# Two-layer cross-attention and FFN network: the second layer's query path staged ahead of the batch loop, with the key rotation on another engine

## Chip, core and metric
One core of a Trainium2 chip. The metric is the device time of one execution in microseconds (us). TensorE is called PE (its weight loads PEld), VectorE DVE, ScalarE ACT, GpSimd POOL, SyncE SP.

## What is computed
`x` is (8, 100, 256), `ctx` (8, 1444, 64). Layer 0 is a causal cross-attention with 16 small heads and a top-1 expert FFN with a shared expert. Layer 1, which the change touches, is below (16 heads, K = 128, query width 192, key width 64); layernorms stand ahead of each block and residuals behind. In the kernel all weights behind the rotation are merged beforehand: `wqb`, `wqt` (query, 128 and 64 of the 192 rows), `amat` (rotated query to 64 latent values that meet the rotated keys), `bmat` (output).

```python
q = (hidden_q @ Wq.T) per head;  q_big = rope(q @ w_kc_q)        # 192 wide
kv_r = rope(kv_c);  q_r = q_big @ W_qr;  k_r = kv_r @ W_kr
scores = q_r @ k_r.T
attn = softmax(scores);  out = (attn @ values(kv_r)) @ Wo.T
x = x + out;  then the FFN of quantised activations and ternary weights
```

## The kernel before
Five instruction streams are written out by hand, one per engine, with semaphores (`wait_ge`, `then_inc`); each engine runs its stream in order. Layer 0, the experts (L1042, L1055) and the merging of weights take the first 255 us. Then comes the stage ahead of layer 1's loop: keys of batch 0 are turned (`turn_keys`, `low_keys`), the shared expert's output is added (`shared_out`, L1008, and `second_residual`), the routed output gathered from DRAM is added (`third_input`, L1923), each batch is normalised (`norm_x3`, with GpSimd's power L636 in between) and turned (`turn_x3`), and the first two units' queries are made.

A unit u is one batch b = u // 2 and one half of the heads (8 heads, 800 query columns). The loop runs over 16 units of 24 slots. In each slot PE computes `scores` (L1197, one of 12 key tiles by 400 query columns, a pair of single-record matmuls: high part and low part), ACT takes the exponent (L1674), and GpSimd adds the weights up, one add of 800 columns per two slots (`add_weights`, L614). Slots 1 to 21 also hold one of 21 `max_chunk`s (L1177) of the next unit, which DVE reduces (L1976); `max_chunk` m waits until reduce m - 2 is done, since there are two banks. Behind slots 7, 15 and 23 stand four `values` each (L1209), a burst on PE of some 2.9 us. `sum_weights`, a reciprocal through DRAM scratch (`spread_sums` on SP), `divide` (L1997, slot 15) and `attention_out` (L1232, slots 17 to 20 of even units) belong to the unit or batch before, as does the FFN: `quantise_x` behind slot 23 of even units, `gate` and `up` in odd ones, `hidden` and `max_h` (L2044) at the end of odd ones. `turn_max` (L1183) at slot 23 ends a unit's slots.

The query path, for unit u + 2 inside unit u: `q_big` (24 matmuls of 100 columns, L1116 and L1121, at slots 1, 3, 5 and 9, 11, 13), `rope` on DVE (L1943, L1947, slots 7 and 15), `q_latent` (24 matmuls, L1143, slot 23), then ACT's `keep_q` (high part, L1592) and DVE's `low_q` (the rest, L1957) in the first slot of the next unit. `turn_x3` and `norm_x3` of batch b + 2 are in the loop too. GpSimd rotates the keys of batch b + 2 (`rotate_keys`, four instructions L594 to L597 for two of 12 tiles, behind slots 7, 15, 23, 31, 39, 47 of batch b). SP loads the raw keys, stores and loads the sums, places the maxima (`place_max`) and stores the output.

Of the kernel before, what the change touches and what calls it, by code (L numbers as in the profile page):

```python
# [84 lines left out]
X_SLOT, NORM_SLOT = 39, 31  # L85
# [11 lines left out]
ROTATE_SLOT = (7, 15, 23, 31, 39, 47)  # L97

# [19 lines left out]
def key_rows(t):  # L118
    return KP if t < KL else KP - 1
# [40 lines left out]
def build(nc, x, ctx_in, wq0, wkv0, wout0, router, gate_up, down, sh_gate, sh_up, sh_down,  # L160
          wq1, kcq, kckv, wqr, wkr, wo1, fg, fu, fd, lnw, rope_q, rope_kc, rope_ks, out):
    with ExitStack() as ctx:
# [30 lines left out]
        ropeq = place("ropeq", [128, 4, S])  # L193
# [76 lines left out]
        assert cursor[0] <= after_qb  # L270
        cursor[0] = after_qb
# [48 lines left out]
        edn = [place(f"edn{i}", [128, FM, D]) for i in range(EBUF - 1)]  # L320
        hs = place("hs", [128, FM, T])
# [21 lines left out]
        for i in range(2):  # L343
# [54 lines left out]
        var2_ready, rstd2_ready, xn2_ready, xn2_turned, xn2_kept = (  # L398
            sem("var2_ready"), sem("rstd2_ready"), sem("xn2_ready"), sem("xn2_turned"), sem("xn2_kept"))
# [102 lines left out]
        def place_max(sp, u):  # L502
# [17 lines left out]
        def _(sp):  # L520
# [64 lines left out]
        def rotate_keys(pool, step, b, j):  # L585
# [1657 lines left out]
```

## Time and profile before

| what | us |
|---|---|
| median of three runs | 905.37 |
| lowest, highest | 898.53, 906.08 |
| profiled execution: span from first to last instruction | 903.0 |
| first scores of the loop | 306.1 |

The profile is one execution on the chip. Busy times of PE rest on modelled ends and overlap, so differences of starts are the surer measure. An fp32 matmul shows as two records. PEclk is the granted clock as a share of 2.4 GHz: 1.00 or 0.50.

### The profile page before, as it was taken

How to read it: one execution, taken by the hardware profiler on the slowest of the kernel's cores; microseconds unless marked ns; L12 is line 12 of the kernel's file. 1: busy time of each engine (PE TensorE's matmuls, PEld its weight loads, DVE VectorE, ACT ScalarE, POOL GpSimd, SP SyncE). 2: the span in 40 equal slices, each digit the busy share in tenths (PEclk: the TensorE clock that was granted, in tenths of full speed). 3: DMA queues.
4: the chain of work that ended last, by engine and by line, in shares of the span. 5: the costliest groups of instructions: out<-in, count | busy, mean ns of one | idle time of the engine just before them, and what ended most of it. 6: DMA issues, size and time to landing. Idle time of an engine off the chain costs nothing.

```text
span 903.0 us, 15604 instructions
## 1 busy us (share of the span) xinstructions
PE 826.4 (92%) x5844; PEld 606.6 (67%) x5844; DVE 585.3 (65%) x1133; ACT 397.2 (44%) x883; POOL 453.2 (50%) x465
## 2 busy tenths in 40 slices
PE   4998879999998799999999999999999999999883
PEld 3566656788887667677667677676767766765442
DVE  3437864213358675677878778778787787786545
ACT  2248852222231454544544454454354454444441
POOL 3000002800041187768776876776776776567630
PEclk9979996999999899999999999999999999999986
DMA  9532022789810100000000100000000000000000
GB/s 212 187 123 89 2 67 79 261 299 317 299 46 10 35 1 12 18 10 10 19 10 1 31 10 2 10 26 7 10 23 10 10 6 10 2 16 10 2 13 11
DMA packets 42168, 52.28 MB, mean 58 GB/s; under 512 B 12230, under 2 KB 35704, under 8 KB 41836
## 3 DMA queue, kind: packets, MB, share of 16 engines
q1 hardware_dynamic: 41068, 49.63, 17.5%
q0 software_dynamic: 1024, 1.64, 0.6%
q8 instruction: 47, 0.77, 0.3%
q14 instruction: 29, 0.24, 0.1%
HBM read 45.80 MB, written 5.36 MB: 57 GB/s over the span
## 4 chain that ended last, share of the span: by engine, by line
PE 68%; DVE 13%; ACT 7%; DMA 5%; issue 5%; SPq 1%; POOL 0%; POOLq 0%; ACTq 0%; DVEq 0%
PE ps L1197 14%; PE ps L1209 10%; PE ps L1177 7%; PE ps L1116 6%; PE ps L1121 3%; PE ps L1232 3%; DMA xs<-xs_scratch 3%; PE ps L1042 3%; PE ps L994 3%; PE ps L1143 3%; ACT sm L1465 2%; PE ps L1055 2%; DVE xyz L1947 2%; DVE xyz L1943 1%; PE ps L893 1%
## 5 line engine op out<-in xcount | busy, mean ns | idle before, releaser
L614 POOL TENSOR_TENSOR acc<-acc,pt 120x800 f32<-120x800 f32 (+1 forms) x157 | 299.1, 1905 | 94.4 <-ACT pt L1674 61.4
L1674 ACT ACTIVATE pt<-ps 120x400 f32<-120x400 f32 (+1 forms) x384 | 190.1, 505 | 222.5 <-PE ps L1197 211.6
L1976 DVE TENSOR_REDUCE nm<-ps 128x1 f32<-128x482 f32 (+1 forms) x336 | 213.7, 655 | 100.3 <-PE ps L1177 98.1
L1197 PE MATMUL ps<-qh,khl 128*120 128x400 f32 (+1 forms) x384 | 157.9, 411 | 11.1 <-ACT pt L1674 8.3
L1209 PE MATMUL ps<-pt,kv 120*64 120x400 f32 (+1 forms) x768 | 143.8, 510 | 0.0
L1177 PE MATMUL ps<-khl,qh 128*128 128x482 f32 (+1 forms) x336 | 131.6, 393 | 5.3 <-DVE nm L1976 4.6
L1197 PE MATMUL ps<-ql,kh 65*120 65x400 f32 (+1 forms) x384 | 134.3, 350 | 0.0
L1197 PEld LDWEIGHTS ps<-qh,khl 128*120 128x120 f32 (+1 forms) x384 | 70.9, 185 | 58.6 <-issue 32.4
L1209 PEld LDWEIGHTS ps<-pt,kv 120*64 120x64 f32 (+1 forms) x768 | 51.9, 138 | 65.8 <-issue 55.8
L636 POOL TENSOR_TENSOR rstd<-veps,mhalf 100x1 f32<-100x1 f32 (+2 forms) x20 | 13.4, 670 | 158.1 <-DVE veps L1808 114.6
L1197 PEld LDWEIGHTS ps<-ql,kh 65*120 65x120 f32 (+1 forms) x384 | 71.3, 186 | 5.1
L1116 PEld LDWEIGHTS ps<-x3T,wqb 128*128 128x128 f32 x512 | 68.3, 195 | 3.1 <-issue 0.7
L614 POOL TENSOR_TENSOR acc<-pt,pt 121x800 f32<-121x800 f32 x16 | 30.6, 1910 | 77.0 <-ACT pt L1674 77.0
L1177 PEld LDWEIGHTS ps<-khl,qh 128*128 128x128 f32 (+1 forms) x336 | 60.1, 179 | 12.6 <-DVE nm L1976 8.9
L1116 PE MATMUL ps<-x3T,wqb 128*128 128x100 f32 x512 | 67.3, 275 | 0.7 <-ACT x3T L1429 0.5
L1042 PE MATMUL ps<-xsT,egu 128*128 128x128 f32 x448 | 52.6, 276 | 1.0 <-DVE hs L1900 0.6
L1042 PEld LDWEIGHTS ps<-xsT,egu 128*128 128x128 f32 x448 | 51.9, 192 | 1.8 <-ACT xsT L1429 1.3
L1592 ACT ACTIVATE qh<-ps 64x400 fp32r<-64x400 f32 x64 | 31.9, 499 | 46.6 <-PE ps L1143 46.1
L689 POOL DMA_INDIRECT xn<-ys_scratch,slot x8 | 8.5, 1067 | 78.2 <-DMA ys_scratch<-ysb 76.2
L1947 DVE TENSOR_TENSOR xyz<-ps,ropeq 64x200 f32<-64x200 f32 x128 | 46.2, 361 | 1.3
L1908 DVE TENSOR_TENSOR hT<-sg,ps 128x512 f32<-128x512 f32 x14 | 9.6, 686 | 48.2 <-PE ps L1042 48.2
L1232 PE MATMUL ps<-bmat,ct 128*100 128x256 f32 x128 | 33.5, 385 | 6.4 <-DVE ct L1997 5.8
(277 smaller groups left out, 1246.0 us busy)
## 6 DMA issues: line engine op xcount, KB each, us to landing
egu<-_L_ffn_gate_up_proj_dram SPq DMA_DIRECT2D x14, 1024.0 KB, 6.0
edn<-in_L_ffn_down_proj_dram SPq DMA_DIRECT2D x14, 512.0 KB, 7.1
spread<-inv_scratch SPq DMA_DIRECT2D x30, 100.0 KB, 2.7
craw<-in_ctx_dram SPq DMA_DIRECT2D x8, 360.0 KB
wo_n<-in_L_xattn_Wo_dram SPq DMA_DIRECT2D x1, 2048.0 KB, 10.5
wq_n<-in_L_xattn_Wq_dram SPq DMA_DIRECT2D x1, 2048.0 KB, 8.0
xs_scratch<-zero SPq DMA_DIRECT2D x1, 1792.0 KB, 9.9
xs<-xs_scratch SPq DMA_DIRECT2D x14, 128.0 KB, 6.1
```

The source lines that it names most:

```text
L614: nc.gpsimd.tensor_tensor(total[r, :, :], before[r, :, :], pt[j % PT_BUF][r, :, :], ALU.add).then_inc(p_added, 1)
L994: last = mm(ps[:, 2 * (k % 2) + a, 0:HT], sgu[:, c, a, 128 * m:128 * m + 128], xnT[:, c, HT * n:HT * n + HT], start=c == 0, stop=c == DC - 1)
L1042: last = mm(ps[:, 2 * (t % 2) + a, TR * m:TR * m + TR], egu[t % EBUF][:, c, FI * a + 128 * m:FI * a + 128 * m + 128], xsT[t % 2][:, c, :], ...
L1116: mm(ps[:, q_bank(u, a), S * part:S * part + S], wqb[:, c, h, 0:128], x3T[:, c, :], start=c == 0, stop=c == DC - 1)
L1177: mm(ps[0:w, 3 + m % 2, 0:MN], qh[u % 2][:, 128 * i:128 * i + w], khl[b % 2][:, MSTART[n]:MSTART[n] + MN], start=True, stop=True).then_inc ...
L1197: last = mm(ps[0:key_rows(t), k % 2, 0:HT], lhs[:, keys], rhs[:, HT * a:HT * a + HT], start=first, stop=not first)
L1209: last = mm(ps[CD * a:CD * a + CD, 2, 0:HT], kv[b % KV_BUF][r, t, :], pt[j % PT_BUF][r, a, :], start=t == 0, stop=t == KT - 1)
L1232: last = mm(ps[0:S, 6, 0:D], ct[:, S * i:S * i + S], bmat[:, i, :], start=i == 0, stop=i == GH - 1)
L1592: last = nc.scalar.activation(qh[u % 2][p:p + CD, HT * a:HT * a + HT], ps[CD * a:CD * a + CD, 5, 0:HT], ACT.Copy)
L1674: nc.scalar.activation(pt[j % PT_BUF][0:rows, k % 2, :], ps[0:rows, k % 2, 0:HT], ACT.Exp).then_inc(p_ready, 1)
L1947: last = tt(o[CD * j:CD * j + CD, 2, e:HG:2, :], ps[CD * e:CD * e + CD, bank + 1, 0:HT // 2].rearrange("p (i q) -> p i q", i=HG // 2), rop ...
L1976: nc.vector.tensor_reduce(nm3[0:w, i, n:n + 1], ps[0:w, 3 + m % 2, 0:MN], AX.X, ALU.max).then_inc(m_reduced, 1)
```

## The change
The query path leaves the loop. It runs ahead of it in eight quads: `quad(n)` gives g (four batches), p (half of the heads) and e (which half of these). A quad is two `q_tail` (L1121's part, two matmuls of 400 columns each), four `q_main` (two each), four `rope`s on DVE (two 128x400 products each; the 64-row tail goes through ACT's `keep_tail` and GpSimd's `rope_tail`), and `q_latent` of the quad before (12 matmuls of 400 columns). `keep_q` and `low_q` write `qhi`, `qlo`; `store_q` writes them to DRAM scratch in four DMAs per quad, `load_q` reads one unit in three (two copies of the high part, one of the low part), into three buffers `qh`, `ql`. `load_q(0)` and `load_q(1)` stand on SP behind `store_q(3)`, `load_q(u + 2)` at the head of unit u. All eight x3 are made ahead of the loop. `max_chunk`s of unit 0 stand in quads 4 to 6. In the loop DVE rotates the keys at the slots where GpSimd did.

```diff
-X2_LATE, X2_DONE, PT_LATE = (2, 3, 4), 9, 2 * 7
-QB_AT = (1, 3, 5)
+HB = B // 2
+QUADS = 2 * NU // HB
+QBUF = 3
+MAIN_BANK, TAIL_BANK, LATENT_BANK = (0, 1), (6, 7), (2, 5)
+TERNARY_IN, X3_IN, MAX_IN = (0, 0, 2, 2, 3, 3), (1, 1, 2, 2), (4, 5, 6)
...
+def quad(n):
+    return n // 4, n // 2 % 2, n % 2
...
+        def store_q(sp, n):
+            g, p, e = quad(n)
+            sp.wait_ge(q_hi, 2 * n + 2)
+            sp.wait_ge(q_lo, 2 * n + 2)
+            heads = q_dram.rearrange("(g b p) l d (a e n) -> g p l a e d b n", g=2, b=HB, p=PAIRS, a=2, e=2)
+            for l, src in enumerate((qhi[e], qlo[e])):
+                for a in range(2):
+                    sp.dma_start(heads[g, p, l, a, e],
+                                 src[CD * a:CD * a + CD, :, :, :].rearrange("d b i s -> d b (i s)").bitcast(F32)).then_inc(q_stored[e], 16)
+        def load_q(sp, u):
+            n = 2 * PAIRS * (u // PAIRS // HB) + 2 * (u % PAIRS)
+            for e in range(2):
+                sp.wait_ge(q_stored[e], 64 * (n // 2 + 1))
+            if u == QBUF - 1:
+                sp.wait_ge(latent_done, 2 * QUADS)
+            elif u >= QBUF:
+                sp.wait_ge(s_done, LANE * (u - QBUF + 1))
+            for p in (0, CD):
+                sp.dma_start(qh[u % QBUF][p:p + CD, :].bitcast(F32), q_dram[u, 0]).then_inc(ld_q[u % QBUF], 16)
+            sp.dma_start(ql[u % QBUF][0:CD, :].bitcast(F32), q_dram[u, 1]).then_inc(ld_q[u % QBUF], 16)
...
-            place_max(sp, 0)
+            for n in range(4):
+                store_q(sp, n)
+            load_q(sp, 0)
+            load_q(sp, 1)
             sp.wait_ge(fq_turned, 6)
...
+            store_q(sp, 4)
+            store_q(sp, 5)
+            place_max(sp, 0)
+            store_q(sp, 6)
+            store_q(sp, 7)
             for u in range(NU):
                 b = u // PAIRS
+                if u + 2 < NU:
+                    load_q(sp, u + 2)
...
+            def rope_tail(n, a, i):
+                m = 4 * n + 2 * a + i
+                pool.wait_ge(tail_kept, m + 1)
...
+                nc.gpsimd.tensor_tensor(zt[m % 8][:, :].rearrange("p (b q) -> p b q", b=HB), tail2[i][:, :].rearrange("p (b q) -> p b q", b=HB),
+                                        ropeq[:, 2, :].unsqueeze(1).to_broadcast([128, HB, S]), ALU.mult).then_inc(z_ready, 1)
...
+            for e in range(2):
+                pool.wait_ge(q_stored[e], 64 * QUADS // 2)
...
-                    if b + 2 < B and s in ROTATE_SLOT:
-                        rotate_keys(pool, step, b + 2, ROTATE_SLOT.index(s))
...
+            def q_tail(n, a):
...
+                for c in range(DC):
+                    last = mm(ps[:, TAIL_BANK[a], 0:HT], wqt[:, c, h:h + 2, :].rearrange("p h q -> p (h q)"),
+                              x3T[:, c, HT * g:HT * g + HT], start=c == 0, stop=c == DC - 1)
...
+            def q_main(n, a, i):
+                g, p, e = quad(n)
+                m = 4 * n + 2 * a + i
+                if m >= 2:
+                    pe.wait_ge(rope_done, m - 1)
+                h = 2 * HG * p + HG * a + 2 * e + i
+                for c in range(DC):
+                    last = mm(ps[:, MAIN_BANK[i], 0:HT], wqb[:, c, h, 0:128], x3T[:, c, HT * g:HT * g + HT],
+                              start=c == 0, stop=c == DC - 1)
+                last.then_inc(main_done, 1)
...
                 if c == 0:
-                    pe.wait_ge(q_hi, u + 1)
+                    pe.wait_ge(ld_q[u % QBUF], 48 * (u // QBUF + 1))
...
+            for n in range(QUADS):
+                q_tail(n, 0)
+                q_tail(n, 1)
+                if n:
+                    q_latent(n - 1)
+                for a in range(2):
+                    for i in range(2):
+                        q_main(n, a, i)
+                        if n in MAX_IN:
+                            for c in range(MC):
+                                if c // 7 == MAX_IN.index(n) and c % 7 // 2 == 2 * a + i:
+                                    max_chunk(0, c)
...
+            def rotate_loop_keys(b, j):
...
+                tt(kcos[r, :, :], c[r, t, :], ropekc[r, t, :], ALU.mult)
+                tt(ksin[r, :, 0:h], c[r, t, h:CD], ropeks[r, t, 0:h], ALU.mult)
+                step(tt(ksin[r, :, h:CD], c[r, t, 0:h], ropeks[r, t, h:CD], ALU.mult))
+                tt(k[r, t, :], kcos[r, :, :], ksin[r, :, :], ALU.add).then_inc(kv_ready, 1)
...
+            dve.wait_ge(ld_rope, 80)
+            dve.wait_ge(tails_set, 2)
+            for n in range(QUADS):
+                if n:
+                    low_q(n - 1, 0)
+                    low_q(n - 1, 1)
+                for a in range(2):
+                    for i in range(2):
+                        rope(n, a, i)
...
                     if b + 1 < B and s in LOW_KEY_SLOT:
                         low_keys(b + 1, LOW_KEY_SLOT.index(s))
+                    if b + 2 < B and s in ROTATE_SLOT:
+                        rotate_loop_keys(b + 2, ROTATE_SLOT.index(s))
                     if u and at == INVERT_AT:
                         invert_sums(u - 1)
```

## Rows read from the trace of the kernel before

**Rows 1.** The page's busy times: us, share of the span, instructions.

```profile
PE 826.4 (92%) x5844; PEld 606.6 (67%) x5844; DVE 585.3 (65%) x1133; ACT 397.2 (44%) x883; POOL 453.2 (50%) x465
```

**Rows 2.** The chain that ended last, by engine.

```profile
PE 68%; DVE 13%; ACT 7%; DMA 5%; issue 5%; SPq 1%; POOL 0%; POOLq 0%; ACTq 0%; DVEq 0%
```

**Rows 3.** Busy times by stretch: stretch, length, engines' busy us, granted clock, DMA.

```profile
255.30:306.10 50.80, 41.95 (x344) 32.98 (x343) 36.53 (x83) 15.63 (x26) 12.41 (x13) 1.00 0.08 23
306.10:312.80 6.70, 6.67 (x24) 6.41 (x25) 3.55 (x11) 2.02 (x4) 0.46 (x1) 0.50 0.36 109
...
658.60:696.80 38.20, 37.23 (x252) 27.07 (x251) 30.02 (x54) 18.91 (x40) 27.02 (x25) 1.00 0.07 19
```

**Rows 4.** Timeline, turns of the maxima: start us, length, engine, line; ends of five units.

```profile
658.58 0.28 PE L1183 MATMUL ps<-ident,nmx 128*7 128x128 f32 x1
...
696.75 0.28 PE L1183 MATMUL ps<-ident,nmx 128*7 128x128 f32 x1
...
731.88 0.28 PE L1183 MATMUL ps<-ident,nmx 128*7 128x128 f32 x1
...
804.75 0.28 PE L1183 MATMUL ps<-ident,nmx 128*7 128x128 f32 x1
...
838.23 0.28 PE L1183 MATMUL ps<-ident,nmx 128*7 128x128 f32 x1
```

**Rows 5.** Groups by line: busy us, mean ns | idle before, releaser.

```profile
L614 POOL TENSOR_TENSOR acc<-acc,pt 120x800 f32<-120x800 f32 (+1 forms) x157 | 299.1, 1905 | 94.4 <-ACT pt L1674 61.4 <-issue 17.0 <-POOL kv L597 8.6
L1976 DVE TENSOR_REDUCE nm<-ps 128x1 f32<-128x482 f32 (+1 forms) x336 | 213.7, 655 | 100.3 <-PE ps L1177 98.1
...
L1116 PE MATMUL ps<-x3T,wqb 128*128 128x100 f32 x512 | 67.3, 275 | 0.7 <-ACT x3T L1429 0.5 <-DVE xyz L1947 0.2
...
L1143 PE MATMUL ps<-xyz,amat 128*64 128x100 f32 x768 | 37.2, 252 | 0.8 <-DVE xyz L1947 0.8
...
L1943 DVE TENSOR_TENSOR xyz<-ps,ropeq 128x400 f32<-128x400 f32 x64 | 33.4, 562 | 0.9 <-PE ps L1121 0.7
```

**Rows 6.** Timeline ahead of the loop: shared expert's gates (L994), then layer 1's first matmuls.

```profile
158.31 0.50 ACT L1538 ACTIVATE sg<-ps 128x400 f32<-128x400 f32 x1 [2.18 <-PE ps L994]
...
161.00 0.50 ACT L1538 ACTIVATE sg<-ps 128x400 f32<-128x400 f32 x1 [2.18 <-PE ps L994]
...
262.46 1.89 PE L1008 MATMUL ps<-sdn,hs 128*100 128x256 f32 x8
...
265.77 2.00 PE L1116 MATMUL ps<-x3T,wqb 128*128 128x100 f32 x16 [0.52 <-ACT x3T L1429]
```

**Rows 7.** Timeline of the loop, units 12 to 14.

```profile
662.04 2.86 PE L1209 MATMUL ps<-pt,kv 120*64 120x400 f32 x16
...
704.60 1.90 DVE L1976 TENSOR_REDUCE nm<-ps 128x1 f32<-128x482 f32 x3
...
714.02 0.41 PE L1197 MATMUL ps<-qh,khl 128*120 128x400 f32 x1
...
722.60 2.91 PE L1209 MATMUL ps<-pt,kv 120*64 120x400 f32 x16
...
812.57 1.90 DVE L1976 TENSOR_REDUCE nm<-ps 128x1 f32<-128x482 f32 x3
...
829.46 1.63 DVE L1997 TENSOR_TENSOR ct<-ctu,spread 128x400 f32<-128x400 f32 x1 [2.51 <-DMA spread<-inv_scratch]
```

**Rows 8.** DMA issues: KB each, median us from issue to landing.

```profile
spread<-inv_scratch SPq DMA_DIRECT2D x30, 100.0 KB, 2.7
...
ys_scratch<-ysb SPq DMA_DIRECT2D x14, 128.0 KB, 6.1
```

**Rows 9.** Timeline, `max_h` on DVE, with GpSimd's adds beside it and without.

```profile
661.56 2.40 DVE L2044 TENSOR_TENSOR sg<-h,lnw_b 100x1024 f32<-100x1024 f32 x1
...
859.05 1.23 DVE L2044 TENSOR_TENSOR sg<-h,lnw_b 100x1024 f32<-100x1024 f32 x1
```

More of the change, by code:

```diff
@@ new lines, in q_main, with q_latent @@
+            def q_main(n, a, i):
+                g, p, e = quad(n)
+                m = 4 * n + 2 * a + i
[6 more added lines that the diff above has]
+                last.then_inc(main_done, 1)
+            def q_latent(n):
+                g, p, e = quad(n)
+                pe.wait_ge(rope_done, 4 * n + 4)
+                pe.wait_ge(z_ready, 4 * n + 4)
+                if n:
+                    pe.wait_ge(q_lo, 2 * n)
+                else:
+                    pe.wait_ge(k_kept, 3)
+                for i in range(2):
@@ L1189, in scores @@
                     pe.wait_ge(max_row, 32 * (u + 1))
-                    pe.wait_ge(q_lo, u + 1)
+                    pe.wait_ge(ld_q[u % QBUF], 48 * (u // QBUF + 1))
                 if k >= 2:
@@ L1952, in low_q @@
-            def low_q(u):
-                dve.wait_ge(q_hi, u + 1)
-                for a in range(2):
-                    cols = slice(HT * a, HT * a + HT)
-                    last = tt(ql[u % 2][0:CD, cols], ps[CD * a:CD * a + CD, 5, 0:HT],
-                              qh[u % 2][CD * a:CD * a + CD, cols].bitcast(F32), ALU.subtract)
-                last.then_inc(q_lo, 1)
+                dve.wait_ge(rstd_ready, AFTER_3 + b + 1)
+                if b >= 2:
+                    dve.wait_ge(x3_turned, b - 1)
@@ new lines, in norm_x3, with rope @@
+                ts(xn3[b % 2][:, :], x_sb[:, b, :], mv[:, b, 0:1], rstd[:, b:b + 1], ALU.subtract, ALU.mult).then_inc(xn3_ready, 1)
+            def rope(n, a, i):
+                m = 4 * n + 2 * a + i
+                dve.wait_ge(main_done, m + 1)
+                if n:
+                    dve.wait_ge(latent_done, 2 * n)
+                for j in range(2):
+                    last = tt(xy[a][i][:, j, :].rearrange("p (b q) -> p b q", b=HB),
+                              ps[:, MAIN_BANK[i], 0:HT].rearrange("p (b q) -> p b q", b=HB),
+                              ropeq[:, j, :].unsqueeze(1).to_broadcast([128, HB, S]), ALU.mult)
+                last.then_inc(rope_done, 1)
@@ L1961, in low_keys, with low_q @@
+            def low_q(n, i):
+                dve.wait_ge(q_hi, 2 * n + i + 1)
+                if n >= 2:
+                    dve.wait_ge(q_stored[n % 2], 64 * (n // 2))
+                tt(qlo[n % 2][:, :, i, :], ps[:, LATENT_BANK[i], 0:HT].rearrange("p (b q) -> p b q", b=HB),
+                   qhi[n % 2][:, :, i, :].bitcast(F32), ALU.subtract).then_inc(q_lo, 1)
             def low_keys(b, j):
```

406 lines of the change are left out of this document (195 added, 211 removed).

## The prediction

> **What bounds the kernel now.** I read the page first. TensorE (PE) is busy for 92% of the span of 903 us [rows 1], and the chain that ended last runs through PE for 68% and VectorE (DVE) for 13% of the span [rows 2]. So PE is the first suspect, but a busy share of PE holds matmuls whose modelled ends overlap, so I went on to the table by stretches. It shows the stage ahead of the loop, 255.3 to 306.1 us, and an even unit of the loop (unit 12, 658.6 to 696.8) [rows 3]. A unit is one batch and one half of the heads: 24 slots, in which PE computes scores, maximum chunks of the next unit and, before the change, the query path of the unit after the next. PE is busy for 37.2 of 38.2 us in unit 12, but DVE is too for 30.0 of them. The turns of the maxima, one per unit, gave the units' lengths. Unit 14 is what decided my forecast: the query path is gone from its slots, since no unit 16 exists, and it is a picture of the loop after the change. It took 33.5 us, not 38.2 [rows 4].
>
> **Stage ahead of the loop: the query path.** The trace shows each fp32 matmul as two records (512 for the 256 calls of L1116). Before, one unit's path is 24 matmuls of 100 columns with 128x128 weights and 24 of `q_latent`. L1116 and L1143 are busy for 67.3 and 37.2 us in 16 units [rows 5], L1121 (half as many records as L1116) for half as long, but successive records of L1116 start only 0.11 us apart (16 records in 2.00 us [rows 6]), so a unit costs 48 x 0.11 + 48 x 0.045 = 7.4 us of PE, 118 us in all.
> After, a quad (half of a unit's heads for four batches) is 12 matmuls of 400 columns. The trace has that shape, in another stage: L994, 128x128 weights, 400 columns. There a step of 8 records ends every 2.69 us (158.31 to 161.00 [rows 6]), so 0.336 us each; 24 records are 8.06 us. `q_latent` is 12 matmuls of 400 columns with 64-wide weights in both column halves, which is L1209's form: 16 records in 2.86 us [rows 7], 0.179 each, so 24 are 4.30. A quad is 12.4 us, eight are 98.9. Wider matmuls save 19 us of PE over the whole kernel, and that is all that PE is spared. The rest moves.
>
> **When the stage starts and ends.** The first query matmul starts at 265.77 now, after one batch is normalised; four are wanted then. Before each of the other three stand a shared product (1.9 us [rows 6]), a residual, a third input and a norm on DVE with GpSimd's power in between, 3.3 us per batch in turn, and three more shared products fill the rest: 265.8 + 3 x 3.3 + 2.8 = 278.5. To this come 98.9 of path; 9 us of other PE work that stays in the stage (21 chunks, six ternary turns, four x3 turns); 2 us for the first rope (`dve.wait_ge(tails_set, 2)` stands ahead of it) and behind the last; and 5 us in quads 4 to 6, where DVE has four ropes of 1.06 us (2 x 0.53) and seven reduces of 0.66 [rows 5], 8.9 us, beside 7 us of PE.
> One wait is new. `max_chunk(0, 0)` in quad 4 waits for `ld_q[0]`, PE works in order, and SyncE issues that load only after `store_q(3)`, whose data come out of `q_latent(3)` just before. From the end of that: copy 0.5, subtraction 0.57, four stores and three loads to issue at 0.5 each (3.5), and a landing. The nearest rows are 2.7 us (100 KB) and 6.1 (128 KB) [rows 8]; I take 3.5. That is 8.3 with semaphores, less 1.34 of `q_main(4,0,0)`: PE idles 7 us (bounds 4.5 and 10). Behind it wait all of PE's matmuls and, with them, DVE's ropes. Before, PE idled 2.3 us and did light work ahead of the loop, and the granted clock then was 0.50, the 1.2 GHz level, from 306.1 to 312.8 [rows 3]. I expect one such fall behind the 7 us: 6.8 us at half pace cost 3.4. (The Trainium skill, "TensorE: Matmul & The Clock Gate", its part on the clock gate, has the same two levels and puts the lower one behind idle time; it would give the same 3.4.)
> The loop starts at 278.5 + 98.9 + 9 + 2 + 5 + 7 + 3.4 = 403.8, against 306.1: **97.7 us later**. `store_q(7)` delays GpSimd's first adds by some 4 us; eight weight buffers hide that. `load_q(u+2)` has a unit's time; hidden.
>
> **What the loop gives back.** Not 7.4 us a unit. Unit 14 shows why: after the last query work DVE still has the FFN's hidden and maximum steps, and its first reduce of the unit starts at 812.57, 7.8 us into the unit; in unit 13 it is 704.60, 7.9 us after 696.75 [rows 4, 7]. PE can run only two chunks ahead of it, so the 2.1 us of `q_latent` and the first `q_big` pieces lie beside a DVE that ends later; removing them is free of effect. After that PE is paced by the reduce, 0.66 per slot, where its own work is two score records of 400 columns and a chunk of 482, some 0.58 by the 0.179 above.
> Even units (4 to 12, five): unit 14's 33.5 plus three key turns with DVE's `low_keys` (0.65 each), 1.2 us beyond cover: 34.7, against 38.17. Gain 3.5.
> Odd units (5 to 13, five), 35.13 now [rows 4]: first eight slots 1.2; the second eight take 8.58 (714.02 to 722.60 [rows 7]) and then 8 x 0.66 + 0.8 = 6.1, gain 2.5; last eight 0.2. Gain 3.9.
> Units 0 to 3 have little or no FFN, so the path's time is nearly all freed: 6.8 (3.4 of it that the clock's fall is not there), 6.5, 6.8, 5.2, together 25.3. Units 13 and 14 keep `low_q` away and rotate nothing: 2.4. Sum 17.5 + 19.5 + 25.3 + 2.4 = **64.7 us**. Bounds: 50, if ScalarE's exponents set the pace at slots that PE now reaches sooner, and 85, if the first reduce moves up with PE.
>
> **The keys on DVE.** 36 rotations of four instructions leave GpSimd (10.8 us a batch; it has idle time, so its relief is worth nothing) and go to DVE, behind slots 7, 15 and 23 of each unit. Alone one is 1.1 us: four at 0.15 to 0.3 us, from 1.23 us for 1024 columns [rows 9], and two waits. The bursts of values on PE (2.9 us) would hide it, and `low_q`'s 1.15 us goes. But DVE does not work alone. L2044, with two SBUF inputs, took 1.23 us with GpSimd quiet and 2.40 while one of GpSimd's adds was running [rows 9]. Such an add takes 1.9 us [rows 5]. So each rotation's first instruction waits for the add in hand, and the next may wait for another. Bounds: nothing, and 7.6 us (four adds) per rotation. GpSimd gets an add per 1.3 us in slots and is behind when a burst begins, so I take one to two adds, 3.7 us a rotation: hidden behind slot 7, 2.5 us too long at slot 15 of an even unit, where `divide` and then `attention_out` wait (the spread already lands late in unit 14: ct idles 2.51 [rows 7]), 1.2 in an odd one; behind slot 23 GpSimd's backlog is merely paid earlier. Some 20 us in the eleven units, of which DVE's order gives back a part: **15 us**.
> The Trainium skill ("GPSIMD Engine Reference", Specifications) says the SBUF interfaces are shared with VectorE, with contention for DVE instructions with two SBUF inputs. The trace agrees by those two rows. By the rule alone every one of the 144 instructions contends; without it the term is zero.
>
> **Sum.** 97.7 - 64.7 + 15 = +48. The profiled execution has a span of 903.0, the runs a median of 905.4 (898.5 to 906.1): 905.4 + 48 = **953 us**. A run can be told from no change here at about 1%, 9 us.
>
> **Rivals.** (A) Faster: PE bounds every stretch. The stage would cost 80 us (no load wait, no fall, no DVE quads), the loop free 14 x 7.4 + 3.4 = 107: 878 us. For it: PE's 92%. Against it: unit 14. It decides if a unit loses more than 5.8 us. Chance 0.06.
> (B) The load lands under other work and the rotations slip between adds: 97.7 - 10.4 - 64.7 = +23, 928 us. For it: GpSimd is busy for half of the span only [rows 1]. Against: the order of SyncE's queue. Chance 0.22, of which 0.05 within 1% of before.
> (C) GpSimd takes the port again after every DVE instruction; two more adds, less what bursts hide, 2 us at the 24 rotations behind slots 15 and 23: +48 more, 1000 us. For it: GpSimd's backlog. Against: it would soon be drained. Chance 0.12.
> Forecast: 0.60. **Range** 915 to 985: it takes in the bounds of the landing, of the loop's gain and half of B's and C's sides. Faster by over 1% 0.06, within 1% 0.05, slower 0.89.
>
> **What would show it.** First scores between 395 and 410; PE idle some 7 us in quad 4 released by a DMA into qh or ql, and clock 0.5 behind it; quads some 12.4 us apart; reduces that still release PE's chunks; units of 34 to 36 us at b >= 2, even ones with `attention_out` waiting on ct; DVE instructions of the rotation well over 0.3 us beside adds. Wrong it would be if units came to 31 us or less, or if 400-column matmuls ran at under 0.3 us a record.

## The result, and the profile after the change

| | before | after |
|---|---|---|
| median of the runs, us | 905.73 (898.53 to 906.46, 4 runs) | 964.66 (959.03 to 968.12, 4 runs) |
| span of the profiled execution, us | 903.0 | 966.3 |
| time after / time before | | 1.066 (95%: 1.061 to 1.072) |

The change made the kernel slower by 59 us, 6.6%. The forecast was 953 us, with a range of 915 to 985. The profile of experiment 1 below is of the longest of its four executions (939.7 us; the others took 920.5 to 933.0), at a lower mean clock.

Two rows of the page after the change, the busy times and the chain that ended last, answer to [rows 1] and [rows 2]:

```profile
PE 843.3 (87%) x4692; PEld 544.6 (56%) x4692; DVE 615.2 (64%) x1133; ACT 403.8 (42%) x899; POOL 429.4 (44%) x358
...
PE 60%; DVE 21%; ACT 7%; issue 6%; DMA 5%; SPq 1%; POOL 1%; POOLq 0%; DVEq 0%; ACTq 0%
```

PE's share of the chain fell from 68% to 60% and DVE's rose from 13% to 21%, while the span grew: on the chain PE has about 34 us less and DVE about 86 us more.

The experts' stage ends at a different time in each execution (247 to 261 us in the profiles of this study, in all but experiment 7 with the same instructions in it), so the stages are compared from one common point: the end of the last matmul of the experts' down projection. The next rows are the busy times by stretch of the kernel before, from that point: up to the first score, the loop, the tail (columns: stretch, length, busy us of PE, PEld, DVE, ACT, POOL with instructions, granted clock, DMA share, GB/s).

```profile
255.70:306.10 50.40, 41.55 (x342) 32.68 (x341) 36.53 (x83) 15.63 (x26) 12.41 (x13) 1.00 0.07 21
306.10:866.00 559.90, 542.22 (x3612) 387.06 (x3612) 417.50 (x790) 271.22 (x559) 398.23 (x331) 0.99 0.04 13
866.00:903.00 37.00, 21.90 (x108) 11.71 (x106) 14.90 (x37) 10.37 (x21) 3.07 (x3) 0.77 0.02 6
```

The same view of the kernel after: the rest of the normalising, the eight quads, the loop, the tail; then single stretches: one in the fifth quad, one in unit 0, the start of unit 7 and what is left of that unit.

```profile
256.50:280.70 24.20, 19.30 (x86) 13.03 (x84) 12.49 (x38) 6.49 (x13) 11.93 (x14) 0.86 0.15 40
280.70:406.90 126.20, 113.30 (x464) 55.78 (x462) 58.28 (x114) 46.35 (x90) 37.09 (x37) 0.96 0.22 59
406.90:930.00 523.10, 468.13 (x2262) 288.58 (x2260) 412.51 (x721) 240.97 (x499) 337.93 (x186) 0.94 0.11 30
930.00:966.30 36.30, 20.80 (x103) 11.07 (x102) 15.28 (x37) 10.12 (x21) 3.06 (x3) 0.79 0.02 6
343.60:353.80 10.20, 5.04 (x9) 3.18 (x10) 2.39 (x5) 0.00 (x0) 0.00 (x0) 0.50 0.72 198
418.70:428.90 10.20, 5.89 (x19) 4.89 (x20) 7.90 (x12) 2.93 (x6) 5.92 (x4) 0.50 0.00 0
644.00:650.80 6.80, 6.66 (x25) 4.96 (x27) 3.75 (x7) 2.24 (x5) 2.16 (x2) 0.50 0.01 2
650.80:669.60 18.80, 18.15 (x94) 10.85 (x90) 15.39 (x28) 9.51 (x18) 12.74 (x7) 1.00 0.05 13
```

From the common point to the first score it was 50.4 us and is 24.2 + 126.2 = 150.4: 100.0 more. Loop and tail were 596.9 and are 559.4: 37.5 less. Together +62.5. Three things are to be seen in the loop's row. DVE is busy for 412.5 us of it, as much as before (417.5), although it lost all the ropes of the query path. GpSimd lost its rotations (398 to 338) and nothing came of it. And PE's clock is at 0.94 of 2.4 GHz where it was at 0.99.

**The wait in the fifth quad, and one in unit 0.** Timeline after the change, stores and loads on SyncE's queue and the PE instruction that waits for them:

```profile
341.65 1.33 SPq L555 DMA_DIRECT2D q_scratch<-qlo  x2
343.41 1.17 SPq L568 DMA_DIRECT2D qh<-q_scratch  x2
344.62 0.60 SPq L569 DMA_DIRECT2D ql<-q_scratch  x1
...
348.76 1.18 PE L1259 MATMUL ps<-khl,qh 128*128 128x482 f32 x2 [8.10 <-DMA ql<-q_scratch]
...
413.06 0.59 SPq L512 DMA_DIRECT2D craw<-in_ctx_dram  x1
...
418.45 1.66 DVE L2061 TENSOR_TENSOR kcos<-craw,ropekc 121x128 f32<-121x128 f32 x1 [4.08 <-DMA craw<-in_ctx_dram]
...
423.01 0.77 PE L1259 MATMUL ps<-khl,qh 128*128 128x482 f32 x1 [5.97 <-DVE nm L2073]
```

The first load of the queries is issued at 343.41, behind the stores of the fourth quad, as the forecast had followed them; PE stands for 8.1 us. The second wait was not in the forecast. The third batch's keys are asked for at 413.06 only, behind the last store and a query load, and the first rotation on DVE stands for 4.1 us until they land. The reduces queue behind that rotation, and PE behind the reduces: 6.0 us. The clock is at 0.50, the 1.2 GHz level, around each of the two, for 10.2 us (the rows 343.60:353.80 and 418.70:428.90 above).

**The start of an odd unit.** Timeline after, DVE, GpSimd and PE at the start of unit 7 (its predecessor's turn of the maxima is at 634.67):

```profile
636.32 2.37 DVE L2064 TENSOR_TENSOR kv<-kcos,ksin 120x128 f32<-120x128 f32 x1
636.66 4.05 POOL L678 TENSOR_TENSOR acc<-acc,pt 120x800 f32<-120x800 f32 x2
...
640.90 1.87 POOL L678 TENSOR_TENSOR acc<-pt,pt 121x800 f32<-121x800 f32 x1 [0.20 <-ACT pt L1765]
641.52 1.40 DVE L2122 TENSOR_SCALAR xq<-xn 100x256 bf16<-100x256 f32 x1
...
643.44 1.21 DVE L2073 TENSOR_REDUCE nm<-ps 128x1 f32<-128x482 f32 x2
644.14 0.77 PE L1259 MATMUL ps<-khl,qh 128*128 128x482 f32 x1 [3.91 <-DVE nm L2073]
```

The last instruction of a rotation takes 2.37 us; the same takes 0.29 with GpSimd nearly quiet (experiment 4). It began 0.34 us before the first of the two additions, and still ends at 638.69, 0.15 us behind the end of that addition (638.54, inside the merged row). Then comes the quantising of x; its last step takes 1.40 us instead of 0.28 (there too) and ends 0.15 behind GpSimd's 642.77. So the first reduce starts 8.8 us into the unit, PE stands for 3.9 us, and then works for 6.8 us at the 1.2 GHz level (the row 644.00:650.80 above). In the kernel before the loop had such a stretch at its beginning only [rows 3], and one near its end.

### The profile page after: what moved, and what is told of

It reads as the page before. It is cut to its first block, busy times and chain, and to the rows that moved or that the text cites. A ratio compares the mean times of both kernels' runs of the same rounds, so it can differ in the third digit from the quotient of the medians.

```text
span 966.3 us, 13320 instructions
## 1 busy us (share of the span) xinstructions
PE 843.3 (87%) x4692; PEld 544.6 (56%) x4692; DVE 615.2 (64%) x1133; ACT 403.8 (42%) x899; POOL 429.4 (44%) x358
## 4 chain that ended last, share of the span: by engine, by line
PE 60%; DVE 21%; ACT 7%; issue 6%; DMA 5%; SPq 1%; POOL 1%; POOLq 0%; DVEq 0%; ACTq 0%
PE ps L1279 10%; PE ps L1291 8%; PE ps L1259 6%; PE ps L1121 4%; DVE nm L2073 4%; PE ps L1205 4%; PE ps L1222 3%; PE ps L1312 3%; PE ps L1073 3%; PE ps L1134 2%; ACT sm L1538 2%; PE ps L1193 2%; DMA xs<-xs_scratch 2%; DVE ksin L2063 2%; PE ps L1087 1%
## 5 line engine op out<-in xcount | busy, mean ns | idle before, releaser
L2073 DVE TENSOR_REDUCE nm<-ps 128x1 f32<-128x482 f32 (+1 forms) x336 | 211.3, 652 | 81.8 <-PE ps L1259 79.8
L1259 PE MATMUL ps<-khl,qh 128*128 128x482 f32 (+1 forms) x336 | 144.0, 431 | 50.5 <-DVE nm L2073 39.3
L1279 PE MATMUL ps<-qh,khl 128*120 128x400 f32 (+1 forms) x384 | 161.0, 419 | 11.3 <-ACT pt L1765 10.2
L1279 PE MATMUL ps<-ql,kh 65*120 65x400 f32 (+1 forms) x384 | 139.6, 364 | 0.0
L1279 PEld LDWEIGHTS ps<-qh,khl 128*120 128x120 f32 (+1 forms) x384 | 74.6, 194 | 70.1 <-ACT pt L1765 31.9
L1259 PEld LDWEIGHTS ps<-khl,qh 128*128 128x128 f32 (+1 forms) x336 | 65.0, 194 | 74.1 <-DVE nm L2073 52.7
L700 POOL TENSOR_TENSOR rstd<-veps,mhalf 100x1 f32<-100x1 f32 (+1 forms) x25 | 16.5, 662 | 166.9 <-DVE veps L1895 114.6
L773 POOL TENSOR_TENSOR zt<-tail,ropeq 128x400 f32<-128x400 f32 x32 | 33.2, 1042 | 76.7 <-ACT tail L1502 75.7
L1121 PE MATMUL ps<-xsT,egu 128*128 128x128 f32 x448 | 52.6, 276 | 1.0 <-DVE hs L1987 0.6
L1121 PEld LDWEIGHTS ps<-xsT,egu 128*128 128x128 f32 x448 | 51.9, 192 | 1.8 <-ACT xsT L1502 1.3
L1205 PE MATMUL ps<-x3T,wqb 128*128 128x400 f32 x128 | 49.0, 523 | 1.2 <-DVE xy L2029 1.2
L1502 ACT ACTIVATE tail<-ps 64x400 f32<-64x400 f32 x64 | 31.9, 498 | 37.3 <-PE ps L1193 32.6
L753 POOL DMA_INDIRECT xn<-ys_scratch,slot x8 | 8.4, 1052 | 78.8 <-DMA ys_scratch<-ysb 77.1
L2061 DVE TENSOR_TENSOR kcos<-craw,ropekc 120x128 f32<-120x128 f32 (+1 forms) x36 | 40.7, 1129 | 4.1 <-DMA craw<-in_ctx_dram 4.1
L2039 DVE TENSOR_TENSOR qlo<-ps,qhi 128x400 fp32r<-128x400 f32 x16 | 9.2, 574 | 49.5 <-ACT qhi L1672 49.5
L2029 DVE TENSOR_TENSOR xy<-ps,ropeq 128x400 f32<-128x400 f32 x64 | 33.7, 568 | 10.8 <-PE ps L1205 8.6
```

The source lines that it names most:

```text
L773: nc.gpsimd.tensor_tensor(zt[m % 8][:, :].rearrange("p (b q) -> p b q", b=HB), tail2[i][:, :].rearrange("p (b q) -> p b q", b=HB), ropeq[: ...
L1121: last = mm(ps[:, 2 * (t % 2) + a, TR * m:TR * m + TR], egu[t % EBUF][:, c, FI * a + 128 * m:FI * a + 128 * m + 128], xsT[t % 2][:, c, :], ...
L1205: last = mm(ps[:, MAIN_BANK[i], 0:HT], wqb[:, c, h, 0:128], x3T[:, c, HT * g:HT * g + HT], start=c == 0, stop=c == DC - 1)
L1259: mm(ps[0:w, 3 + m % 2, 0:MN], qh[u % QBUF][:, 128 * i:128 * i + w], khl[b % 2][:, MSTART[n]:MSTART[n] + MN], start=True, stop=True).then_ ...
L1279: last = mm(ps[0:key_rows(t), k % 2, 0:HT], lhs[:, keys], rhs[:, HT * a:HT * a + HT], start=first, stop=not first)
L1502: return nc.scalar.activation(dst, src, ACT.Copy, **more)
```

## The experiments

"From the common point" below is the span less the end of the experts' last down matmul: 647.3 us before, 709.8 after. It leaves out the part that scatters.

**1. Keys rotated on GpSimd again.**

```
 (GpSimd, loop)
+                    if b + 2 < B and s in ROTATE_SLOT:
+                        rotate_keys(pool, step, b + 2, ROTATE_SLOT.index(s))
 (VectorE, loop)
-                    if b + 2 < B and s in ROTATE_SLOT:
-                        rotate_loop_keys(b + 2, ROTATE_SLOT.index(s))
```

> The changed kernel with the key rotation of the loop given back to GpSimd, at the same slots; the query path ahead of the loop stays. Theory 1 (the rotations on VectorE, slowed beside the adds, delay the first reduces of the odd units, PE then waits and its clock falls): the units of the loop end in about 31 us on even and odd ones alike, the 3.9 us waits at the start of the odd units and the clock falls behind them are gone, 925 to 950 us. Theory 2 (the waits come from the quantising of x and the reduces themselves, and the loop has lost the query matmuls that kept PE's clock up): 958 to 970 us, odd units still 34 to 35 us, clock still at 0.50 in most units.

Measured: 930.4 us (ratio to before 1.024, 1.016 to 1.033); from the common point 677.9, 31.9 less than after the change. The even units take 32.1 us and the odd ones 31.4 to 32.7. Theory 1 holds for the time; its units of 31 us and its steady clock did not come: waits of 1.5 to 2.9 us at the start of the odd units stay, with stretches of 3.4 to 6.8 us at 0.50 behind them.

**2. That part alone, in the kernel before.** `rotate_keys` goes from GpSimd's loop to VectorE's, ahead of `invert_sums`, with its waits.

> The kernel before with that one part of the change: the rotation of the keys in the loop on VectorE instead of GpSimd, everything else as before. Theory 1: each rotation takes 3 to 4 us beside the adds where it would take 1.0 alone, and the loop is longer by 15 to 35 us: 920 to 940 us. Theory 2: the loop of before has slack for it, because the query path's matmuls cover it: 901 to 911 us.

Measured: 980.8 us (1.082, 1.076 to 1.089), 75 us slower; from the common point 729.5, +82.2. More than either theory said. By stretch, loop and tail:

```profile
311.20:953.30 642.10, 574.89 (x3612) 405.49 (x3612) 495.63 (x934) 271.29 (x559) 338.92 (x187) 0.94 0.04 11
```

DVE is busy for 78 us more than in the loop of before (417.5), and the loop is 82 us longer: in this loop PE waits 20.0 us for reduces (2.1 before), 15.3 for `ct` (5.8) and 22.2 for the ropes of the query path (about 1). In the changed kernel the same rotations cost 32. That the ropes, which have left that loop, make the difference fits these waits, but no run took the ropes away alone.

**3. Two DMA issues earlier.**

```
-            for n in range(4):
-                store_q(sp, n)
+            store_q(sp, 0)
+            store_q(sp, 1)
             load_q(sp, 0)
+            store_q(sp, 2)
+            store_q(sp, 3)
             load_q(sp, 1)
+            load_keys(sp, 2)
```

> The changed kernel with two DMA issues of SyncE earlier: the first unit's query load right behind the two stores that it reads, and the third batch's keys loaded ahead of the loop. If the 8.1 us wait of PE in the fifth quad and the 6.0 us wait in unit 0 are as the chain shows them, both go and so do the two stretches of 10.2 us at half clock behind them (about 5 us each): 940 to 951 us. If VectorE's reduces or another store end last in their place: 956 to 963 us.

Measured: 947.9 us (1.048, 1.041 to 1.055), 17 us less than after. The quads and the loop by stretch:

```profile
274.40:390.40 116.00, 111.06 (x464) 54.35 (x462) 57.98 (x114) 46.34 (x90) 37.09 (x37) 1.00 0.26 68
390.40:907.00 516.60, 464.11 (x2258) 284.47 (x2256) 413.19 (x721) 240.63 (x498) 338.02 (x186) 0.95 0.11 30
```

The eight quads take 116.0 us instead of 126.2, with PE busy for 111.1 of them and the clock at 1.00: no reduce and no store took the place of the load. From the common point the run is 18.0 us shorter. Loop and tail give 5.2 of it, nearly all in unit 0, where PE's wait of 6.0 us shrank to 2.0. The last 2.6 lie in the normalising ahead, which the edit doesn't touch (21.6 us at full clock here, 24.2 at 0.86 after the change).

**4. GpSimd's additions nearly left out.** All but the first addition of a unit take 8 columns a head group instead of 400, so most weights are missing from the sums.

```
-            nc.gpsimd.tensor_tensor(total[r, :, :], before[r, :, :], pt[...][r, :, :], ALU.add)
+            n = HT if t == 1 else 8
+            nc.gpsimd.tensor_tensor(total[r, :, 0:n], before[r, :, 0:n], pt[...][r, :, 0:n], ALU.add)
```

> The changed kernel with GpSimd's additions of the softmax weights cut to 8 columns a head group (all but the first of each unit), which leaves most of the weights out of the sums. Theory 1 (two engines with two SBUF operands each share the port): a rotation on VectorE takes 1.0 to 1.3 us instead of 3.0, and the odd units lose their wait: 930 to 950 us. Rival (the rotation is slow by itself in the loop, whatever GpSimd does): 2.5 to 3.0 us each and 958 to 967 us.

Measured: 911.8 us (1.007, 1.003 to 1.010), 53 us less than after. It lies below the band of theory 1 (930 to 950): the instructions are as long as theory 1 says, the gain is larger. Groups by line after the change (busy us, mean ns | idle before), the four instructions of a rotation, the division and the last step of the quantising:

```profile
L2061 DVE TENSOR_TENSOR kcos<-craw,ropekc 120x128 f32<-120x128 f32 (+1 forms) x36 | 40.7, 1129 | 4.1 <-DMA craw<-in_ctx_dram 4.1
L2063 DVE TENSOR_TENSOR ksin<-craw,ropeks 120x64 f32<-120x64 f32 (+1 forms) x36 | 33.0, 918 | 0.0
L2064 DVE TENSOR_TENSOR kv<-kcos,ksin 120x128 f32<-120x128 f32 (+1 forms) x36 | 20.9, 582 | 1.2
L2094 DVE TENSOR_TENSOR ct<-ctu,spread 128x400 f32<-128x400 f32 x15 | 12.0, 803 | 1.3 <-DMA spread<-inv_scratch 1.2
L2122 DVE TENSOR_SCALAR xq<-xn 100x256 bf16<-100x256 f32 x8 | 10.2, 1280 | 0.0
L2062 DVE TENSOR_TENSOR ksin<-craw,ropeks 120x64 f32<-120x64 f32 (+1 forms) x36 | 7.7, 213 | 0.0
```

The same groups with the small additions:

```profile
L2065 DVE TENSOR_TENSOR kv<-kcos,ksin 120x128 f32<-120x128 f32 (+1 forms) x36 | 10.5, 292 | 1.2
L2062 DVE TENSOR_TENSOR kcos<-craw,ropekc 120x128 f32<-120x128 f32 (+1 forms) x36 | 10.1, 279 | 4.3 <-DMA craw<-in_ctx_dram 4.3
...
L2063 DVE TENSOR_TENSOR ksin<-craw,ropeks 120x64 f32<-120x64 f32 (+1 forms) x36 | 7.8, 216 | 0.0
L2064 DVE TENSOR_TENSOR ksin<-craw,ropeks 120x64 f32<-120x64 f32 (+1 forms) x36 | 7.8, 215 | 0.0
L2123 DVE TENSOR_SCALAR xq<-xn 100x256 bf16<-100x256 f32 x8 | 2.3, 284 | 0.0
```

A rotation takes 279 + 216 + 215 + 292 = 1.00 us beside a quiet GpSimd and 1129 + 213 + 918 + 582 = 2.84 us beside its additions, as the two rows of [rows 9] had shown for one instruction. That is 66 us in 36 rotations; DVE's whole busy time falls from 615.2 to 531.2. The clock in the loop is at 0.99 again. So the collision is the cause of the loop's loss. Not all of the 53 us belong to the rotations, since the division, the quantising and `max_h` get shorter too. How much 36 us of DVE work cost beside a quiet GpSimd isn't isolated: this loop takes 472.5 us with them, and that of experiment 7, without rotations but with all additions, 475.4.

**5. Repairs 1 and 3 together.**

> Both repairs together in the changed kernel: keys rotated on GpSimd in the loop as before, and SyncE's query load of the first unit and key load of the third batch issued early. If the two costs are separate ones, their gains add (34 and 17 us): 908 to 918 us. If early loads only moved the wait in unit 0 that a DVE rotation had caused, the second gain shrinks to that of the fifth quad (8 us and its half clock, 10 us or so): 919 to 925 us.

Measured: 915.0 us (1.015, 1.004 to 1.026). From the common point 658.3: 51.5 less than after, against 31.9 + 18.0 for the two alone (experiment 3 has 691.8 from there). The time is in the band of the first answer, but the stretches show that the second is half true. Here are normalising, quads, loop and tail, two stretches in the loop, and then unit 0, from the first score to the turn of the maxima that ends it, here, in experiment 1 and in experiment 3:

```profile
248.50:272.70 24.20, 19.27 (x85) 13.01 (x83) 12.52 (x38) 6.50 (x13) 11.94 (x14) 0.86 0.15 41
272.70:388.70 116.00, 111.05 (x463) 54.33 (x461) 57.98 (x114) 46.41 (x90) 37.12 (x37) 1.00 0.25 68
388.70:872.20 483.50, 452.30 (x2267) 276.29 (x2265) 335.64 (x577) 242.24 (x502) 396.89 (x331) 0.98 0.12 32
872.20:906.80 34.60, 19.64 (x98) 10.43 (x98) 14.78 (x36) 8.87 (x18) 2.20 (x3) 0.79 0.02 6
540.50:543.90 3.40, 3.40 (x17) 2.81 (x16) 2.26 (x4) 1.74 (x4) 3.04 (x2) 0.50 0.00 0
604.40:607.80 3.40, 3.35 (x25) 2.11 (x25) 2.75 (x5) 2.15 (x5) 3.26 (x2) 1.00 0.02 5
...
388.71:411.50 22.79, 22.09 (x115) 14.31 (x113) 15.79 (x26) 14.92 (x30) 14.66 (x11) 1.00 0.23 63
...
410.37:433.18 22.81, 22.11 (x116) 14.30 (x114) 15.78 (x26) 14.90 (x30) 14.70 (x12) 1.00 0.31 79
...
390.38:416.27 25.89, 22.59 (x115) 14.40 (x113) 22.16 (x35) 14.90 (x30) 17.07 (x9) 1.00 0.20 55
```

The fifth and sixth row follow the start of units 5 and 7, where PE waited 1.75 and 1.77 us for the first reduce: once the clock fell, once it did not.

Unit 0 took 30.7 us after the change and takes 25.9 in experiment 3. With the keys on GpSimd it takes 22.8, whether the key load is early or not. So the late key load costs time only where a rotation on DVE waits for it, with DVE's reduces behind. Beside keys on GpSimd, early loads gain the 10.2 us of the quads. Loop and tail are another 9.4 us shorter than in experiment 1 (518.1 against 527.5), but 8.3 of these lie in the odd units 5 to 13, where the clock is at 0.50 for 27.2 us in experiment 1's profile and for 6.8 in this one. That is a difference between two executions, and no effect of the loads is shown in it.

**6. The rotations on VectorE at other slots.** On top of experiment 3:

```
-ROTATE_SLOT = (7, 15, 23, 31, 39, 47)
+ROTATE_SLOT = (5, 13, 21, 29, 37, 43)
```

> The changed kernel with early loads, its rotations still on VectorE but each a few slots away from the ends of the units: slots 5, 13, 21, 29, 37, 43 of a batch instead of 7, 15, 23, 31, 39, 47, so that none stands between the last reduce of one unit and the first of the next. Theory place (a rotation costs where it makes the first reduce late; elsewhere PE has work ahead): the 3.9 us waits at the start of the odd units shrink to under 2 us, their half clock goes, 925 to 940 us against 948 with the old slots. Theory load (VectorE has lost 72 us to collisions and is the bound of the units wherever they stand): within 5 us of 948.

Measured: 963.8 us (1.069, 1.062 to 1.077): 16 us worse than with the old slots. Theory place falls, and so does theory load in its plain form. Away from the bursts of values the four instructions take 900 + 475 + 1203 + 698 ns = 3.28 us instead of 2.86 (experiment 3), the odd units still begin with a wait of 4.0 us, and every other unit now ends with one of 1.9 us for the last reduce. What a rotation costs depends on how many additions it meets, and of the two sets of slots that were tried, 7, 15 and 23 is the one where GpSimd is less in the way.

**7. No rotation in the loop.** On top of experiment 3, GpSimd rotates the keys of batches 2 to 7 in place before the loop (two batches behind the first two, four between its steps of the quads), SyncE stores them to a DRAM scratch and loads them in each even unit:

```
+                        j = 4 * (n % 2) + 2 * a + i
+                        if j < KT // 2:
+                            rotate_keys(pool, step, 4 + n // 2, j)
...
+                if u % PAIRS == 0 and b + 2 < B:
+                    load_turned(sp, b + 2)
```

> The changed kernel with early loads and with no key rotation in the loop on either engine: GpSimd rotates batches 2 to 7 before the loop, in its idle time beside the experts and the query stage, through a DRAM scratch, and SyncE loads them in the loop. If the loop is then bound by PE (as in the run with small additions, 30.3 us a unit, and the last two units everywhere): first scores 116 to 122 us behind the first query matmul, units of 30 to 31 us, 885 to 905 us. If the even units have another limit of about 32.1 us, which they showed both with small additions and with the keys on GpSimd: 905 to 920 us.

Measured: 919.4 us (1.022, 1.016 to 1.027); from the common point 654.6, in the profiled execution. The even units stay at 32.1 us, the odd ones fall to 29.8 to 31.1. So the second answer: the even units have a limit of their own near 32.1 us that neither engine's rotations set. It is for the most part PE's own work: PE is busy for 30.6 us of an even unit (the row 698.09:730.20), which holds the turns of the keys and `attention_out`, and for 27.6 of an odd one. The quads take 120.1 us here instead of 116.0. PE is busy for 448 of the loop's 475 us (clock 0.99); there is little left to take.

```profile
404.90:880.30 475.40, 448.14 (x2267) 272.78 (x2265) 335.06 (x577) 241.69 (x502) 336.44 (x187) 0.99 0.12 34
...
668.25:698.09 29.84, 27.58 (x145) 16.47 (x145) 21.39 (x41) 14.60 (x30) 21.29 (x12) 1.00 0.15 41
698.09:730.20 32.11, 30.59 (x155) 19.19 (x154) 24.62 (x40) 16.76 (x35) 21.47 (x13) 1.00 0.11 30
```

**8. Shorter additions.** On top of experiment 3, each addition in two halves:

```
-            nc.gpsimd.tensor_tensor(total[r, :, :], before[r, :, :], pt[...][r, :, :], ALU.add).then_inc(p_added, 1)
+            nc.gpsimd.tensor_tensor(total[r, 0, :], before[r, 0, :], pt[...][r, 0, :], ALU.add)
+            nc.gpsimd.tensor_tensor(total[r, 1, :], before[r, 1, :], pt[...][r, 1, :], ALU.add).then_inc(p_added, 1)
```

> The changed kernel with early loads, each addition of GpSimd (1.91 us) issued as two of half the columns, the same elements in all. Theory lock (a VectorE instruction with two SBUF operands stands until the GpSimd instruction in flight ends): the longest wait falls from 1.9 to about 1.0 us, the first multiplication of a rotation from a mean of 1.1 us to about 0.65, the second ksin one from 0.92 to about 0.55, and the time from 948 to 925 to 942 us. Theory shared bandwidth (both engines go at a lower rate while both read SBUF): the traffic is the same, the means stay within 0.1 us and the time within 5 us of 948; or, if each half lets GpSimd come between two of VectorE's instructions more often, the rotations get longer and the time goes above 953.

Measured: 939.9 us (1.040, 1.035 to 1.045) against 947.9, and these groups:

```profile
L2068 DVE TENSOR_TENSOR kv<-kcos,ksin 120x128 f32<-120x128 f32 (+1 forms) x36 | 32.1, 893 | 1.2
L2067 DVE TENSOR_TENSOR ksin<-craw,ropeks 120x64 f32<-120x64 f32 (+1 forms) x36 | 27.0, 751 | 0.0
L2065 DVE TENSOR_TENSOR kcos<-craw,ropekc 120x128 f32<-120x128 f32 (+1 forms) x36 | 22.5, 626 | 0.0
L2066 DVE TENSOR_TENSOR ksin<-craw,ropeks 120x64 f32<-120x64 f32 (+1 forms) x36 | 16.9, 470 | 0.0
...
L2126 DVE TENSOR_SCALAR xq<-xn 100x256 bf16<-100x256 f32 x8 | 3.8, 469 | 0.0
```

The first multiplication falls from 1.11 to 0.63 us and the last step of the quantising from 1.29 to 0.47, though the elements added are the same: the wait follows the length of the instruction in flight. That is a lock and no shared rate. The other half of the rival came too. GpSimd, with more instructions to start, takes the port between DVE's more often (the second instruction from 0.26 to 0.47 us, the fourth from 0.58 to 0.89), so the rotation as a whole only falls from 2.86 to 2.74. And not every wait is halved: the long ones of the fourth instruction at the start of the odd units went from 2.38 to 2.52 us, since both halves pass ahead of it, and the waits of PE there stay at 3.9 to 4.0 us in units 5 to 11.

**9 and 10. The halves elsewhere:** on top of experiment 5, and in the kernel before.

> Keys on GpSimd, early loads and the additions in halves. VectorE's remaining waits for GpSimd (ct 1.30 us against 0.57 alone, the two steps of the quantising 1.1 and 1.4 against 0.35 and 0.28) shrink by about half, some 2 us a batch: 903 to 912 us against 915. If GpSimd, at about 90% in the loop, is the bound there, the doubled count of its instructions costs 0.05 to 0.1 us each and it is 915 to 925 us.

> The kernel before with the additions in halves. Its loop is bound by PE (94% busy), so that shorter waits of VectorE gain 0 to 6 us: 898 to 905 us. If GpSimd's extra instructions make the sums late: 906 to 912 us.

Measured: 917.9 us (1.011, 1.007 to 1.014) and 902.5 us (0.995, 0.992 to 0.997). With the keys on GpSimd nothing is gained that can be told from 915.0, and the time is in the band of the second answer. In the kernel before it is 3.4 us, small, but the interval excludes no change, and it is the one version here that is faster than both kernels: `max_h`'s 2.19 us became 1.82 and the last step of the quantising 0.49 instead of 1.24.

## Why the prediction was right, and where its terms were off

The direction and the size were right (+48 forecast, +59 measured), by the reasons it gave: the query path ahead costs about 100 us, the loop gives back less than that, and the keys collide with GpSimd's additions. From the common point the kernel is 62.5 us longer, 14.5 more than the forecast's 48: the keys cost 17 us more and the stage 2.3, and the loop gave back 4.7 more, so that the errors in part cancel. Term by term, with the units counted from 0 (the stretches that the prediction calls units 12 and 13, 658.6 to 731.9 us, are units 10 and 11; the kinds, even and odd, are as it says):

- **The stage ahead, 97.7 forecast, 100.0 measured.** The first query matmul came at 280.7 (278.5 forecast), the wait for `ld_q[0]` was 8.1 us (7), the first score 406.9 (403.8). The second quad took 12.9 us (291.38 to 304.29) where 12.4 were counted: eight records of 400 columns take 2.85 us, 0.356 each, not the 0.336 of [rows 6]. The half clock behind the load wait was 10.2 us long, not 6.8. Experiment 3 confirms the load wait: 10.2 us of the stage went with it.
- **What the loop gives back, 64.7.** This term was made without the keys, and experiment 1 measures it: loop and tail 596.9 before, 527.5 with the keys on GpSimd, 69.4 less. That the sum came so near is partly luck, since its parts were off both ways: the five even units gave 30.4 us where 17.5 were counted, the five odd ones 13.6 where 19.5 were, and units 0 to 3 gave 21.2 where 25.3 were. The reading of unit 14 as a picture of the loop after the change is what failed here. The query work of unit 15 still stood in it: `q_latent` behind the turn of the maxima, and two `low_q` ahead of the first reduce.

```profile
806.09 2.28 PE L1143 MATMUL ps<-xyz,amat 128*64 128x100 f32 x48
...
811.38 1.16 DVE L1957 TENSOR_TENSOR ql<-ps,qh 64x400 fp32r<-64x400 f32 x2
```

  Without them the first reduce of unit 14 starts 6.6 us into the unit and not 7.8, and the unit takes 30.3 us instead of 33.5, in the kernel after and in each of its eight variants alike. PE is busy for 29.4 of the 30.3. So removing `q_latent` was not "free of effect", and such a unit is paced by PE rather than by the reduces. After the change itself unit 0 gave 0.3 us and not 6.8, because of the key load, which the forecast didn't look at: it followed SyncE's queue for the query load only, and not for `load_keys(2)` behind it.
- **The keys on DVE, 15 forecast, 32 measured** (709.8 less 677.9; 33.5 with early loads, 691.8 less 658.3). This is the term that failed. The price of a rotation was set too high (3.7 us taken, 2.84 measured), its effect too low. (The rotations stand in twelve units, 0 to 11, where it says eleven.) The step that failed is "hidden behind slot 7 ... 1.2 in an odd one": PE runs only two chunks ahead of DVE's reduces, and at slots 21 to 23, the end of a batch's even unit, DVE has residual, rotation and quantising in a row. In the odd units the forecast gain of 3.9 us was not there: 35.3, 35.0, 34.2 and 34.2 us in units 5, 7, 9 and 11 against 35.1 before [rows 4], for the first reduce came 0.9 us later than before (8.8 us into the unit, not 7.9) and the wait behind it drew the clock down.
- **The clock.** One fall was forecast. The loop has 13 stretches at 0.50, 65 us in all, that is 32 us of full clock lost, against 7 before (two stretches) and 8.5 in experiment 5 (four). At most some 25 us of the loop's length can be this; PE does not need all of it, and it can't be taken apart from the waits that cause it, since no run holds the clock and keeps the waits.
- **Rival A** (PE bounds all, 878 us) is refuted even with all repairs: the best form of the change is 915.0. **Rival B** (load hidden, rotations between the additions, 928) did not happen: the load was not hidden, though experiment 3 shows that it can be, and the rotations waited. **Rival C** (GpSimd comes in after every DVE instruction) is half true: after the change the second instruction of a rotation never waits, the third does in 15 of 36 and the fourth in 5. With the additions in halves these are 11, 23 and 19, which is nearer to C.

So where did the gain of wider matmuls and an emptier loop go? The rows of before and of experiment 5 tell it without the two accidents. Ahead of the loop PE's busy time grew by 88.8 us (41.6 to 130.3) and the length by 89.8 (50.4 to 140.2): nothing hides there. In loop and tail PE's busy time fell by 92.2 (564.1 to 471.9), but the length only by 78.8 (596.9 to 518.1). The 13.4 us between are time in which PE isn't busy: its waits for the reduces grew from 2.1 to 15.2 us and those for ScalarE's exponents from 8.3 to 12.2, while those for `ct` fell from 5.8 to 0.6. That the query matmuls had filled these waits is an inference. So PE's work fell by 3.4 us in all, and the kernel is 11.0 us longer. The rotations on DVE add 33.5 to it (691.8 less 658.3), and the late loads, beside them, 18.0 (709.8 less 691.8): 62.5.

## What to carry to other kernels

Before work is moved from GpSimd to VectorE, look at what GpSimd is running beside it: an instruction on DVE that wants the shared port costs what is left of the GpSimd instruction in flight (or one that starts just behind it), so that a short one cost four times its own length here (0.28 us alone, 1.13 in the mean), and the order of the two engines' work counts for more than their busy shares. When a stage is hoisted out of a loop in which it had filled waits for other engines, the loop can get back less than the stage costs. And when a stretch is taken as a picture of the loop to come, list its instructions first: the one used here still held some of the work that was to go. And each new DMA on an in-order queue should be followed to all that stands behind it, not only to its own landing.

## What the runs showed of the hardware that was not expected

- **DVE waits for the whole GpSimd instruction.** Of the 36 first multiplications of a rotation (L2061) 30 took over 0.43 us, and every one of the 30 ended 0.15 us behind the end of an addition of GpSimd; the 15 of L2063 that waited all ended 0.08 to 0.09 us behind one, and none of the short ones lay wholly inside an addition. The longest took 1.95 us with additions of 1.91, and 1.10 us with halves of 1.06. The five of the fourth instruction (L2064) that waited had started 0.34 us ahead of an addition, and still waited for all of it, 2.38 us; with halves, for two of them, 2.52 us. The Trainium skill ("SBUF — State Buffer", "SBUF: two separate sides") says that the pair of ports is an exclusive lock, held for a whole instruction, and that the loser is blocked; these ends agree. The forecast had cited the contention without it.
- **Operands decide, also single ones.** Beside the additions the quantising steps with one SBUF operand of 100x256 got longer (L2122 0.28 to 1.28 us, L2114 0.35 to 0.80). A reduce of PSUM (L2073, 652 ns after and 652 with small additions) and one of SBUF (L2109, 100x256, 420 ns in both) did not, though 174 of 315 and 5 of 8 began while an addition ran. The 64x480 subtraction with one operand in PSUM and one in SBUF did not either (649 ns in both, 13 of 14).
- **The second instruction of a rotation mostly goes through, but not by a rule.** After the change L2062 took 208 to 219 ns in all 36; in experiments 3, 6 and 8 the same instruction waited in 1, 5 and 11 of 36. GpSimd waits for DVE too: in experiment 5 an addition took 2.84 us that began 0.15 us behind the start of a `max_h` product of 1.22 us.
- **PE's clock fell behind short waits.** Around each of the four waits of 3.9 us after the change it went to 1.2 GHz for 6.8 us, once with PE busy for 6.66 of them (row 644.00:650.80). In the even units, with waits of 1.6 us, it fell for 3.4 us in units 4, 6 and 8 and not in 10 and 12. In experiment 5 it fell for 3.4 us behind one wait of 1.75 us and not behind another of 1.77. What decides between them no run here shows.
